# Query products and output products of a cross-attention block as two unbroken runs on TensorE

## The reference

```python
q = _layer_norm(query, ln1_g, ln1_b)
qh = (q @ wq + bq).reshape(Bq, Sq, H, hd)
kh = (context @ wk + bk).reshape(Bq, Sc, H, hd)
vh = (context @ wv + bv).reshape(Bq, Sc, H, hd)
scores = jnp.einsum('bqhd,bkhd->bhqk', qh, kh) * scale
scores = jnp.where(allowed[None, None, :, :], scores, NEG_INF)
probs = jax.nn.softmax(scores, axis=-1)
o = jnp.einsum('bhqk,bkhd->bqhd', probs, vh).reshape(Bq, Sq, Dm)
x = query + o @ wo + bo
h = _layer_norm(x, ln2_g, ln2_b)
return x + jax.nn.gelu(h @ w1 + b1, approximate=False) @ w2 + b2
```

## Time and profile before

| | |
|---|---|
| median of 3 runs | 2072.11 us (2072.11 to 2073.61) |
| span of the profiled execution | 2069.1 us |
| PE busy | 1903.2 us (92%), 10694 matmuls |
| DVE busy | 1286.2 us (62%) |
| ACT busy | 584.4 us (28%) |
| POOL busy | 455.0 us (22%) |
| chain that ended last | PE 65%, DVE 16%, issue 6%, DMA 5%, ACT 4% |

### The profile page before, as it was taken

How to read it: one execution, slowest core, us unless ns; L and a number is a source line. 1 busy time by engine, 2 the same in 40 slices (tenths; PEclk the granted TensorE clock), 3 DMA queues, 4 the chain that set the end, 5 groups by cost and what they waited for, 6 DMA issues and landing times.

```text
span 2069.1 us, 27368 instructions
## 1 busy us (share of the span) xinstructions
PE 1903.2 (92%) x10694; PEld 910.3 (44%) x10694; DVE 1286.2 (62%) x1908; ACT 584.4 (28%) x756; POOL 455.0 (22%) x380
## 2 busy tenths in 40 slices
PE   4659999999999999999999999999999999999999
PEld 2224444444444444444444444444444444444444
DVE  5857766656666665666666566676566666566542
ACT  3434423232232312223232232313223231322311
POOL 2431231312213131211412023131122214111210
PEclk7869999999999999999999999999999999999999
DMA  7130201103021120202102030210302021020200
GB/s 259 40 93 1 51 31 34 49 1 61 22 46 36 24 59 1 61 21 45 38 15 68 1 58 24 42 41 7 76 1 57 26 41 42 1 63 19 41 21 21
DMA packets 160761, 84.77 MB, mean 41 GB/s; under 512 B 135656, under 2 KB 137232, under 8 KB 160656
## 3 DMA queue, kind: packets, MB, share of 16 engines
q1 hardware_dynamic: 160656, 83.14, 16.5%
HBM read 31.22 MB, written 16.78 MB: 23 GB/s over the span
## 4 chain that ended last, share of the span: by engine, by line
PE 65%; DVE 16%; issue 6%; DMA 5%; ACT 4%; SPq 2%; DVEq 2%; POOL 0%; POOLq 0%; ACTq 0%
PE ff_ps L1200 22%; PE ff_ps L1001 22%; PE at_ps L1001 15%; DMA arena<-qT 4%; DVE ssum L942 3%; DVE arena L974 3%; PE at_ps L1122 2%; PE at_ps L1044 2%; SPq L399 2%; PE at_ps L1142 2%; DVEq L703 2%; DVE xhat L722 1%; DVE act_T L726 1%; DVE qT L726 1%; DVE arena L726 1%
## 5 line engine op out<-in xcount | busy, mean ns | idle before, releaser
L1200 PE MATMUL ff_ps<-w_all,arena 128*128 128x512 f16 x3072 | 720.5, 385 | 44.4 <-DVE arena L726 39.2
L1001 PE MATMUL ff_ps<-arena,w_all 128*128 128x512 f16 x3072 | 710.1, 382 | 3.6 <-issue 2.0
L1200 PEld LDWEIGHTS ff_ps<-w_all,arena 128*128 128x128 f16 x3072 | 299.7, 99 | 405.4 <-DVE arena L726 46.1
L1001 PEld LDWEIGHTS ff_ps<-arena,w_all 128*128 128x128 f16 x3072 | 297.0, 98 | 358.8 <-issue 23.7
L660 ACT ACTIVATE arena<-ff_ps,b1p,scales 128x512 f32<-128x512 f32 x256 | 198.9, 777 | 814.3 <-PE ff_ps L1001 738.7
L726 DVE SCALAR_TENSOR_TENSOR arena<-arena,scales 128x512 f16<-128x512 f32 x256 | 279.2, 1091 | 9.1
L502 POOL TENSOR_TENSOR arena<-arena,rsum 128x1024 f32<-128x1024 f32 x64 | 123.7, 1964 | 695.3 <-DVE rsum L945 695.3
L438 POOL TENSOR_TENSOR rstd<-ve,minus_half 128x1 f32<-128x1 f32 x128 | 90.6, 708 | 696.8 <-DVE ve L707 689.5
L974 DVE TENSOR_SCALAR arena<-arena,scales 128x512 f16<-128x512 f32 x256 | 160.6, 627 | 77.1 <-ACT arena L660 77.1
L1001 PE MATMUL at_ps<-wo_hi,act_T 128*128 128x512 f16 x512 | 163.7, 382 | 1.5 <-DVE act_T L726 1.5
L1001 PE MATMUL at_ps<-act_T,wq_hi 128*128 128x512 f16 x512 | 152.5, 379 | 4.8 <-DVE act_T L726 4.8
(11 more groups left out here) (131 smaller groups left out, 1471.1 us busy)
## 6 DMA issues: line engine op xcount, KB each, us to landing
x_sb<-in_x SPq DMA_DIRECT2D x64, 256.0 KB, 2.7
out_x<-arena SPq DMA_DIRECT2D x64, 256.0 KB, 2.1
w_all<-in_L_xattn_w SPq DMA_DIRECT2D x6, 1024.0 KB, 15.4
arena<-in_L_xattn_w SPq DMA_DIRECT2D x2, 1024.0 KB, 14.4
v_sb<-v_sb SPq DMA_DIRECT2D x6, 192.0 KB, 3.0
arena<-in_ctx SPq DMA_DIRECT2D x1, 1024.0 KB, 5.7
arena<-in_L_xattn_wk SPq DMA_DIRECT2D x1, 1024.0 KB, 7.8
arena<-in_L_xattn_wv SPq DMA_DIRECT2D x1, 1024.0 KB, 7.6
```

The lines of the kernel that those rows point to most:

```text
L1001: last = nc.tensor.matmul(out_ap, s, m, start=(i == 0), stop=(i == n - 1))
L1200: last = nc.tensor.matmul(ff2_ps[:, t, :], pair[:, s, rows], m[:, j], start=(j == 0 and i == 0), stop=(j == NJ - 1 and i == 2))
```

## The change

Only PLAN changes, and with it slots 1 to 15. The diff in full:

```diff
@@ -52,12 +52,12 @@
 PLAN = {
     2: [("T", 0)], 4: [("T", 1)], 5: [("T", 2), ("T", 3)],
-    6: [("Q", 0)], 7: [("Q", 1)], 8: [("Q", 2)], 9: [("Q", 3)],
-    10: [("S", 0)], 12: [("S", 1)], 13: [("S", 2)], 15: [("S", 3)],
-    16: [("E", 0), ("E", 1), ("E", 2), ("E", 3)],
-    19: [("Z", 0)], 20: [("Z", 1)], 21: [("Z", 2)], 22: [("Z", 3)],
-    23: [("V", 0), ("V", 1)], 25: [("V", 2), ("V", 3)],
-    26: [("O", 0)], 27: [("O", 1)], 28: [("O", 2)], 29: [("O", 3), ("H", 0)],
+    7: [("Q", 0), ("Q", 1), ("Q", 2), ("Q", 3)],
+    9: [("S", 0)], 11: [("S", 1)], 12: [("S", 2)], 14: [("S", 3)],
+    15: [("E", 0), ("E", 1), ("E", 2), ("E", 3)],
+    18: [("Z", 0)], 19: [("Z", 1)], 21: [("Z", 2)], 22: [("Z", 3)],
+    23: [("V", 0), ("V", 1)], 26: [("V", 2), ("V", 3)],
+    27: [("O", 0), ("O", 1), ("O", 2), ("O", 3)], 29: [("H", 0)],
     30: [("H", 1)], 31: [("H", 2)], 33: [("H", 3)],
 }
```

## The result

| | before | after |
|---|---|---|
| median | 2072.11 us | 1992.83 us |
| ratio, with its 95% interval | | 0.9618 (0.9604 to 0.9631) |
| span of the profiled execution | 2069.1 us | 1989.9 us |
| PE busy, share of the span | 92% | 94% |
| slot 2 to 15, mean | 121.9 us | 116.4 us |

The change makes the kernel 3.8% faster, 79.3 us by the medians and 79.2 us by the spans. The time lies 3.8 us above the forecast of 1989 us.

What follows compares the result with a forecast made beforehand. PE, 92% busy, was taken as the bound, so only its waits could shrink: 80.4 us in slots 2 to 15 plus 4.3 in slot 1, less 1.7 for the clock, giving 1989 us; range 1979 to 2014.

Steps and rivals of the forecast that it cites:

- The walk of one slot: Predicted times along the new order from the end of S(3), with durations from slot 8, showing F2(8) and V not waiting.
- The sum: Gains in slots 2 to 15: F2(8) 41.6, V 18.8, Q(0) 5.6, clock at F2(8) 14.4; together 80.4 us.
- 1.7 for the clock: Deduction of 1.7 us from the gain, because the clock may fall a little more often at T(3).
- V, at 18.8 us: V's DMA waits outside slot 0, taken as 16.6 us plus 0.16 us for each of 14 waits, would all go.
- the 25.6 us I named as a sign: In the profile after, V's wait on the DMA would be about 25.6 us, from slot 0 alone.
- 4.3 predicted: Slot 1: of 6.5 us lost at F2(8), 2.2 stay, waiting for a converted weight piece; 4.3 us gained.
- What I called free: Places expected to add no wait: inside the Q and O runs, S(0) behind Q(3), O(0), and the tail.
- The clock rival: Clock falls at F1(3) behind T(3) waits in all slots: 19 us back, 2008 us; chance 0.13, shared with V.
- The prediction's upper bound: Split 8 on DVE with both halves slowed all the way beside POOL: 5.05 us, ending at 14.3.

Runs made afterwards that it cites:

- e3: Kernel before, with only the four Q steps moved to position 7, back to back behind F2(1): 2066.22 us, ratio 0.9960.
- e4: Kernel before, with only the four O steps moved to position 27, back to back, and H(0) alone at 29: 2073.24 us, ratio 0.9995.
- e2: Changed kernel, with the softmax step E put back from position 15 to 16, behind gelu 8 on ACT: 2057.48 us, ratio 0.9932.
- e6: Changed kernel, with T(3) moved from position 5 to 6, behind F1(3): 1965.82 us, ratio 0.9487.
- e8: Kernel of e6, with the run of Q moved from position 7 to 8: 1963.28 us, ratio 0.9478.
- e6_again: Kernel of e6 unchanged, measured once more on the chip of e8: 1967.02 us, ratio 0.9492.
- e1: Kernel before, with only softmax step E moved from position 16 to 15, ahead of gelu 8 on ACT: 2021.45 us, ratio 0.9736.
- e7: Kernel before, with POOL dividing only 2 of the 64 probabilities per head, the rest left undivided: 2026.19 us, ratio 0.9782.

## Why the prediction was right

**The place and the mechanism** held: F2(8) and V in every slot, released late by one chain, and set free by starting the chain earlier on ACT and placing its readers later on PE. The walk of one slot against slot 8 of the changed kernel, in us behind the end of S(3):

| | predicted | measured |
|---|---|---|
| sum 0 starts | 3.85 | 3.7 |
| split 8 ends | 13.5 | 13.5 |
| F2(8) starts | 15.5 | 15.55 |
| Z(0) split | 14.7 | 14.6 |
| Z(1) split | 17.1 | 16.9 |
| V(0), V(1) | 23.3 | 23.4 |
| second pair of V | 32.5 | 32.7 |

**The sum.** For slots 2 to 15 I had 80.4 us, less 1.7 for the clock, and 76.6 came. The mis-sized term is V, at 18.8 us. I took the one long wait of slot 0 out of the line of 42.2 us, but slot 0 has a second one (which is also why V's line stands at 32.1 us after, and not at the 25.6 us I named as a sign):

```profile
113.73 2.77 PE L1142 MATMUL at_ps<-arena 128*64 128x256 f16 x24 [25.56 <-DMA arena<-qT]
120.73 2.77 PE L1142 MATMUL at_ps<-arena 128*64 128x256 f16 x24 [4.23 <-DMA arena<-qT]
```

(kernel before, slot 0). The loop had 42.2 - 25.56 - 4.23 = 12.4 us in 13 waits, with 0.16 us for each 14.5 us. With that the sum is 76.1 us. No run has V's longer gap by itself; its 14.5 us are read from the two traces, in which the waits and the slow blocks of the loop add up to what the loop gained. In slot 1 the wait of F2(8) is 2.48 us (2.2 predicted), without a fall of the clock, and 5.7 us were gained for 4.3 predicted. There luck has a part: F1(3) of slot 1 took 4.44 us before and 2.75 us after, with its order unchanged. So the forecast was 4.3 us too high on V and 3.2 us on slot 0, and 1.7 us too low on the clock and 1.4 us on slot 1: part of its closeness is errors that cancel.

**What I called free** was free: the inside of both runs, S(0) behind Q(3), and the tail. I named the run of Q as worth 5.6 us and the run of O as nothing; e3 and e4 measured 8 and 1 us by the medians, with intervals that hold both.

**The clock rival.** Long rows of F1(3) behind T(3) stand in slots 2 and 6 after (3.95 and 4.44 us), two, as before, in slots 6 and 14. So it neither came nor went with the change. Over the eight kernels that keep T(3) at position 5, F1(3) runs slow in 17 of 112 slots of the loop, all of them even slots, where the wait ahead of T(3) is 1.6 to 2.2 us: 17 of the 37 waits of 1.92 us or more, none of the 19 shorter ones. None of the 56 waits of 1.34 us in the odd slots did it. The granted clock of the changed kernel from 754.3 to 758.8 us, over the slow block of slot 6, is 0.62. Behind the 2.8 us waits of F2(8) the clock fell in 38 of 56 (before, e2, e3, e4). In e6 and e8, which have neither wait, it falls nowhere in the loop. The rule of the Trainium skill ("TensorE: Matmul & The Clock Gate", "A second HAM failure mode: psum-queue depth-cycling"), by which frequent short idles of PE make the clock swing, thus agrees in kind, and the time that it would have given, 2008 us, was not the time.

**The 3.2 us in slot 0.** Its order is unchanged, and yet slot 1 starts at 152.2 us and not at 149.1. Over all the traces of this study it starts between 147.7 and 153.3 us, without following any edit (e6 152.7, e6_again 153.3, e8 148.3), and in slot 0 each engine waits in turn for the first loads and reductions. I take it for a spread of slot 0, which is argued and not shown; nothing here was run to find its cause.

## What to carry to other kernels

Where several in-order engines share one order of work, find the late chain's first movable step and count, in blocks of the bounding engine, how far it is from its readers. Here moving one step ahead of one gelu on ScalarE (e1) gave two thirds of the gain, while the unbroken runs that the change seemed to be about gave one tenth. And when a wait is removed, price the next reader of the same chain anew: what it waited for was partly covered by the wait that is gone.

## What the runs showed of the hardware

- Two DVE instructions on SBUF, 0.48 and 0.75 us alone, take 1.97 and 2.27 us beside POOL's divisions, and 0.42 and 0.75 us when POOL's work is cut away (e7). They last as long as the POOL instruction beside them: the first ends 0.28 us behind the end of the third division and the second 0.55 us behind the end of the fourth, in all 140 slots of the loop in the ten traces with full divisions. The same two distances stand behind POOL's shorter additions (L497, L507), beside which the two take 1.48 to 1.76 us. The prediction's upper bound, the second slowed by the same factor as the first, doesn't describe this. The sums at L942, 1.16 us each, are not slowed by the same divisions.
- After 17 of 37 waits of PE of 1.92 to 2.21 us, and after 38 of 56 of 2.8 us, the granted clock was at the lower level, 1.2 GHz, for a while, which cost a block of 12 matmuls 1.2 to 1.7 us; after 19 waits of 1.61 to 1.91 us and 56 of 1.34 us it did not happen.
- A transposing DMA of one 128-row tile of probabilities lands 4.4 us after its issue (median). Of the pair Z(0), Z(1) the second landed 6.7 to 6.8 us behind the issue of the first, in slots 3 to 15 of five traces (before, after, e1, e2, e7), whether it was issued 1.9 or 2.4 us behind it. What holds it back isn't shown.
